# Normed attention's projections on steps of their own, and one wait for four scores

## The reference

```
k = _ln(x @ Wk.T), q = _ln(x @ Wq.T)      # per head of 16 numbers, 16 heads
v = x @ Wv.T
dot = einsum(q, k) / sqrt(16), causal mask
attn = softmax(dot);  out = einsum(attn, v) @ Wu.T
x = _layernorm(x + out)
```

## Time and profile before

| what | us |
|---|---|
| median of 3 executions | 4183.81 (4180.03 to 4212.95) |
| the profiled execution | 4193.01, its span 4191.2 |
| the stage, first transpose to last norm | about 1632 to 2144 of the span |
| its middle, from batch to batch 26 times | 1689.25 to 2085.85 |
| TensorE, VectorE, ScalarE busy over the span | 77%, 54%, 52% |

### The profile page before, as it was taken

The page is one execution under the profiler, slowest core; times in us unless marked ns, Lnnn a source line. Parts: engine busy times, 40 slices in busy tenths (PEclk is TensorE's granted clock), DMA queues, the critical chain, the costliest instruction groups (busy, mean ns, idle before and its releaser), DMA issues. The chain is left out here.

```text
span 4191.2 us, 84333 instructions
## 1 busy us (share of the span) xinstructions
PE 3225.6 (77%) x21166; PEld 1996.2 (48%) x21166; DVE 2278.8 (54%) x10359; ACT 2184.1 (52%) x6653; POOL 1448.4 (35%) x2228
## 2 busy tenths in 40 slices
PE   7999987888988824887767777877777775687772
PEld 5566665566666512444434444444444444344441
DVE  1222222566666684667648888888888882211112
ACT  3433333566566602666637877877777783221110
POOL 1111111355455545455523444444343441110005
PEclk9999998899999966768767887888888785899996
DMA  1000000111111011000010000000000003206773
GB/s 62 19 12 12 14 15 29 36 38 38 34 37 39 20 38 49 19 19 22 18 38 18 16 18 20 16 18 16 18 19 16 18 8 113 90 33 203 223 228 110
DMA packets 111870, 189.32 MB, mean 45 GB/s; under 512 B 11150, under 2 KB 95886, under 8 KB 105550
## 3 DMA queue, kind: packets, MB, share of 16 engines
q1 hardware_dynamic: 102094, 166.32, 12.9%
q10 hardware_dynamic: 7200, 14.68, 0.9%
q0 software_dynamic: 2400, 6.56, 0.5%
HBM read 149.90 MB, written 37.62 MB: 45 GB/s over the span
## 5 line engine op out<-in xcount | busy, mean ns | idle before, releaser
L3034 DVE MAX8 sa_cand<-sa_s 128x8 f32<-128x45 f32 (+3 forms) x3328 | 404.1, 191 | 34.7 <-ACT sa_s L2880 31.8
L852 ACT ACTIVATE ca_p<-ca_sm,ca_nb 100x361 f32<-100x361 f32 x512 | 301.9, 591 | 210.8 <-DVE ca_nb L936 209.8
L2763 PE MATMUL sa_tr<-sa_ident,sa_s 128*128 128x128 f32 (+3 forms) x1248 | 277.3, 339 | 167.9 <-POOL sa_s L2639 90.8
L672 POOL TENSOR_SCALAR ca_p<-ca_p,ca_rec 100x361 f32<-100x361 f32 x512 | 286.7, 579 | 345.2 <-DVE ca_rec L950 344.9
L2639 POOL TENSOR_SCALAR sa_s<-sa_s,sa_unit,sa_nu 128x361 f32<-128x361 f32 (+1 forms) x416 | 261.3, 644 | 306.3 <-DVE sa_nu L3126 306.3
L2763 PEld LDWEIGHTS sa_tr<-sa_ident,sa_s 128*128 128x128 f32 (+3 forms) x1248 | 185.5, 178 | 268.4 <-issue 257.5
L2888 ACT ACTIVATE sa_s<-sa_s,sa_nt 128x361 f32<-128x361 f32 (+1 forms) x416 | 244.3, 592 | 97.2 <-DVE sa_nt L3087 97.2
L936 DVE CUSTOM_DVE_ANT_0 ca_sm<-ca_sc,ca_mb 100x361 f32<-100x361 f32 x512 | 252.3, 526 | 69.4 <-PE ca_sc L759 56.4
L2896 ACT ACTIVATE sa_spare_a<-sa_s,sa_nu 128x361 bf16<-128x361 f32 (+1 forms) x416 | 247.2, 595 | 64.8 <-DVE sa_nu L3128 64.8
L2629 POOL TENSOR_TENSOR sa_over<-sa_cand,sa_tc 128x280 f32<-128x280 f32 (+3 forms) x128 | 99.3, 776 | 451.6 <-DVE sa_tc L3053 272.8
L2749 PE MATMUL sa_sc<-sa_kT,sa_qm 32*128 32x361 f32 (+3 forms) x768 | 227.2, 522 | 22.1 <-ACT sa_s L2880 21.5
(11 more groups left out here) (323 smaller groups left out, 7755.8 us busy)
## 6 DMA issues: line engine op xcount, KB each, us to landing
ea_we<-m_experts SPq DMA_DIRECT2D x40, 1024.0 KB, 6.6
ea_wd<-m_experts SPq DMA_DIRECT2D x40, 512.0 KB
ca_cTs<-cT SPq DMA_DIRECT2D x32, 361.0 KB
sa_cTs<-cT SPq DMA_DIRECT2D x32, 361.0 KB
rows_in<-me_zeros ACTq DMA_DIRECT2D x1, 7168.0 KB
ea_xe<-rows_in SPq DMA_DIRECT2D x40, 128.0 KB
rows_out<-ea_ye ACTq DMA_DIRECT2D x40, 128.0 KB
ca_ms<-mask SPq DMA_DIRECT2D x32, 141.0 KB
```

The source lines that it names most:

```text
L672: ins = pool.tensor_scalar(p[:, r, j, :], p[:, r, j, :], rec[:, r, j:j + 1], 1.0, ALU.mult, ALU.mult)
L852: act.activation(p[:, r, j, :], sm[:, r % 2, j, :], ACT.Exp, bias=nb[:, r % 2, j:j + 1], scale=-1.0, accum_out=den[:, r, j:j + 1]).then_in ...
L2763: mm = pe.transpose(tr[f % 2][0:kn, c0:c0 + rows], s[0:rows, u, i, k0:k0 + kn], ident[0:rows, 0:rows])
L3034: ins = dve.max(cand[0:rows, i, q, :], s[0:rows, u, i, PART[q]:PART[q + 1]])
```

## The change

Four things are changed, all in `normed_attention`. The projection of k and q moves from step 1 to step 0. The projection of v moves from the end of step 3 to the end of step 2, and its copy on ScalarE with it. The transpose of x moves from step 0 to the end of step 3 and works one batch further ahead (n+3 in place of n+2), for which the loads start a batch earlier and the written-out part of `passes` grows by a batch at the front and two at the back. And the four maxima of a step share one `stand`, on the last of the four scores.

```diff
             return (*shift(m, u, (r - steps) // 4), (r - steps) % 4)
 
         def passes(eng, body):
-            for n in range(-2, 2):
+            for n in range(-3, 2):
                 body(n // 2, n % 2)
-            with eng.Fori(1, B // 2 - 1) as m:
+            with eng.Fori(1, B // 2 - 2) as m:
                 body(m, 0)
                 body(m, 1)
-            for n in range(B - 2, B + 2):
+            for n in range(B - 4, B + 2):
                 body(n // 2, n % 2)
 
         block = ctx.enter_context(nc.Block())
@@ -1423,19 +1423,19 @@
                 sp.dma_start(out_s[n], xn[:, u, :]).then_inc(stored[u].sem, 16)
 
             def body(m, u):
-                if there(m, u, 4):
-                    load(*shift(m, u, 4))
+                if there(m, u, 5):
+                    load(*shift(m, u, 5))
                 if there(m, u, -3):
                     store(*shift(m, u, -3))
                 if there(m, u, 0):
                     load_residual(m, u)
 
-            for n in range(-4, 4):
+            for n in range(-5, 4):
                 body(n // 2, n % 2)
-            with sp.Fori(2, B // 2 - 2) as m:
+            with sp.Fori(2, B // 2 - 3) as m:
                 body(m, 0)
                 body(m, 1)
-            for n in range(B - 4, B + 3):
+            for n in range(B - 6, B + 3):
                 body(n // 2, n % 2)
             for u in range(2):
                 sp.wait_ge(*stored[u].at(B // 2, 0))
@@ -1484,6 +1484,7 @@
                 n = 2 * m + u
                 pe.wait_ge(*xq_in[u].at(m, 1))
                 pe.wait_ge(*v_done.at(n, -1))
+                pe.wait_ge(*xT_done.at(n, 0))
                 for k in range(KD):
                     mm = pe.transpose(mix[:, k * S:(k + 1) * S], xq[:, u, k * P:(k + 1) * P], ident[0:S, 0:S])
                 mm.then_inc(xt_done.sem, 1)
@@ -1505,9 +1506,9 @@
                     mm = pe.transpose(kq[:, k * S:(k + 1) * S], c[:, u, k * P:(k + 1) * P], ident[0:S, 0:S])
                 mm.then_inc(kqT_done.sem, 1)
 
-            def project_v(m, u, ahead):
-                n = 2 * m + u
-                if ahead:
+            def project_v(m, u):
+                n = 2 * m + u
+                if there(m, u, 1):
                     pe.wait_ge(*xT_done.at(n + 1, 1))
                 pe.wait_ge(*z_done.at(n, -2))
                 for k in range(KD):
@@ -1571,14 +1572,15 @@
                     if there(m, u, (r - 3) // 4):
                         values(*lag(m, u, r, 3))
                     if r == 0 and there(m, u, 2):
-                        turn_x(*shift(m, u, 2))
-                    if r == 1 and there(m, u, 2):
                         project_kq(*shift(m, u, 2))
                     if r == 1 and there(m, u, -2):
                         project_out(*shift(m, u, -2))
                     if r == 3 and there(m, u, 1):
                         scores(*shift(m, u, 1), 0)
-                        project_v(*shift(m, u, 1), ahead=there(m, u, 2))
+                    if r == 2 and there(m, u, 1):
+                        project_v(*shift(m, u, 1))
+                    if r == 3 and there(m, u, 3):
+                        turn_x(*shift(m, u, 3))
 
             passes(pe, sequence)
 
@@ -1648,12 +1650,12 @@
                         copy_kq(*shift(m, u, 1))
                     if r % 2 == 0 and there(m, u, (r - 2) // 4):
                         copy_turned(*lag(m, u, r, 2))
-                    if r == 0 and there(m, u, 2):
-                        copy_x(*shift(m, u, 2))
                     if r == 1 and there(m, u, 2):
                         squares(*shift(m, u, 2))
-                    if r == 3 and there(m, u, 1):
+                    if r == 2 and there(m, u, 1):
                         copy_v(*shift(m, u, 1))
+                    if r == 3 and there(m, u, 3):
+                        copy_x(*shift(m, u, 3))
 
             passes(act, sequence)
 
@@ -1686,8 +1688,8 @@
             def maxima(m, u, r):
                 n = 2 * m + u
                 dve.wait_ge(*exp_done.at(n, 4 * r - 12))
+                stand(dve, turns, *sc_done.at(n, 4 * r + 4))
                 for j in range(4):
-                    stand(dve, turns, *sc_done.at(n, 4 * r + j + 1))
                     dve.tensor_tensor_reduce(sm[:, r, j, :], sc[j][0:S, 0:S], cm[:, :], -1 / 4, 3e38, ALU.add, ALU.min,
                                              nb[:, r, j:j + 1]).then_inc(mx_done.sem, 1)
```

## The result

The changed kernel takes 4160.73 us (median of 5, 4154.11 to 4165.09) against 4186.78 us before (median of 5, 4180.03 to 4212.95). The ratio is 0.9927 with a 95% interval of 0.9899 to 0.9955. The forecast was 4148 us, within 4105 to 4192. In the profiled executions the span went from 4191.2 to 4163.3 us.

The account below looks back on a forecast made before the run. A chain to and fro between the engines sets the pace, with TensorE's clock varying. Legs summing to 13.7 to 14.5 us a batch gave 14.1, 36 us off over 31 steps: median 4148 us, range 4105 to 4192.

Parts of the forecast that it names:

- three legs: One batch's chain: first scores to k and q's projection, that projection, then on to the next first scores; 13.7 us half-low.
- One low spell a batch: TensorE's clock falls once a batch; the projection of k and q, first large work behind it, takes 2.5 to 3.5 us.
- the 14.1 chosen: Forecast us a batch in normed attention, the middle of 13.7 and 14.5, 1.15 less than now.
- half-low form: Case with half of k and q's projection at full clock and half at half clock: 13.7 us a batch.
- 0, with 3 us either way: Cost of the written-out batches' added code and some steps at the edges.
- The size of a set: Four maxima on VectorE, first to reciprocal, without register instruction and wait between: 0.74 us.
- the wait for the fourth score: At step 0 the first maximum starts 0.87 us behind the first scores, against 0.60 before; counts once a batch.
- waits were free: Rival, chance 0.06: VectorE's maxima keep their times but start on the fourth score; 14.65 us a batch, 4165 us.
- leg one: First scores to the start of k and q's projection: 3.3 or 3.8 us, 2.5 to 3.1 us off.
- Clock stays up: Rival, chance 0.27: TensorE's clock stays up more; 13.2 us a batch, 4121 us, or 4092 with no low spell.
- TensorE becomes the bound: Rival, chance 0.08: low clock lasts through the projections of k and q and of v; 16.5 us a batch, 4223 us.
- Nothing comes of it: Rival, chance 0.12: k and q's projection is wholly on the chain and new waits cancel gains; 15.25 us a batch, 4184.

Follow-up runs that it names:

- e7: Changed kernel plus two idle 256-column projections a batch, one behind v's projection, one behind the transpose of x; ratio 0.9828 to the kernel before, 12.15 us a batch.
- e10: e7 with a wait of its own for each of a step's four scores; ratio 0.9847 to the kernel before, 12.97 us a batch.
- e11: Kernel before, in its old order, with one wait a step and one idle 256-column projection ahead of step 3's transposes; ratio 0.9905, 13.39 us a batch.
- e1: Kernel before with only the one wait for a step's four scores, nothing moved; ratio 0.9945, 14.90 us a batch.
- e2: Changed kernel with all moves but four waits a step put back; ratio 1.0007 to the kernel before, 15.36 us a batch.
- e5: Changed kernel plus one idle 256-column projection behind v's projection, ahead of step 3's transposes; ratio 0.9944 to the kernel before, 13.68 us a batch.
- e3: Kernel before with one wait a step and only v's projection and copy moved to step 2; ratio 0.9950, 14.79 us a batch.

## Why the prediction was right, and where not

**The bound and the chain.** Right. A chain between the engines set the pace. Its walk came within 0.15 us in each of its three legs at the mixed clock (3.70 + 2.85 + 7.1, forecast 3.8 + 2.7 + 7.2) and within about 0.2 us at the full clock of e7 (3.09 + 1.89 + 7.13, forecast 3.3 + 1.8 + 7.2).

**The clock.** Right. One low spell a batch was expected and the projection of k and q to pay for it: it takes 2.92 to 3.74 us in the changed kernel. The mean, 13.83 us, lies below the 14.1 chosen, since nearly all batches stay in the half-low form. That the clock is the reason was shown by e7: more work, a clock of 1.00, and 1.7 us less a batch. By the rule of the Trainium skill (TensorE: Matmul & The Clock Gate, "Why this matters for your kernels") gaps this short leave the clock up. The trace does not agree: the longest wait of TensorE's matmuls in the list of the changed kernel is 1.3 us, and the projection of k and q still takes 2.92 us or more in every batch.

**The forecast on the median.** 36 us off was the sum. The stage gave 42.8, the rest of the program took 15 back: 14.1 in the sparse attention, 4 in the stages ahead, less 3 elsewhere. The prediction had priced the longer code at "0, with 3 us either way". That term was wrong in a way it had not looked at: the longer code cost nothing in its own stage's edges that shows, but 14.1 us in the next stage. Without them the profiled program would have gained 42 us and not 28. The 4 us ahead are most likely scatter: the first stage, which nothing touches, ends 3.6 us later, and over all profiled executions the first transpose of normed attention lies between 1627.7 and 1642.1 us. That the forecast came within 13 us of the median is in part luck, since the stage gave 7 us more than its 36 and the rest took 15.

**The maxima.** The size of a set, 0.74 us, was right, and the wait for the fourth score smaller than taken (0.73 us and not 0.87). What the waits cost was too small: the rival "waits were free" put 0.55 us a batch on them, e10 measured 0.82. The Trainium skill (VectorE: DVE Perf Modes, "Rules for kernel authors") says to minimise the number of operations, "not sems". e10 does not bear this out for these short operations; here three waits a step, each with its register instruction and its increment, cost 0.2 us, 0.07 us each. The runs don't tell these three apart.

**How the parts share the gain.** Here the reasoning fell short. The prediction added the parts up (2.5 to 3.1 us off leg one and 1.1 onto leg three, with the shorter maxima in both). In the experiments they don't add: in the stage 13.0 us for the one wait, 3.6 for the moves, 42.8 for both. Each shift of the chain also shifts how much of the projection meets the low clock, which the sum left out. It also took 2 us of v's projection as on the chain; at a full clock the whole of the moves is worth 0.1 to 0.3 us a batch (e11), so most of the 1.07 us a batch between e1 and the changed kernel comes through the clock (0.74 and 0.86). e1's expectation (5 to 10 us) and e2's (12 to 19 us lost) both missed, in part for that reason and in part because the waits cost more than taken: 24.4 us of the stage at a full clock (e10 against e7).

**The rivals.** "Clock stays up" and "TensorE becomes the bound" did not come, for the reasons given. "Nothing comes of it" came true for the moves alone (e2).

## What to carry to other kernels

Where TensorE's clock is near one of two levels by stretches, an order of work is worth what it does to the clock: look at which matmuls come first behind a gap. Matmuls without use in the gaps can pay (here 1.7 us of 13.8 a batch), so try that before a reordering, since it also tells how much the clock costs. And measure the parts together as well as alone: two changes of one chain need not add up. Last, look at the stages behind the changed one too: here 14 of the 43 us that the stage gained were lost there again, and 10 of them came back when VectorE's code was moved.

## What the runs showed that was not expected

- The clock fell although TensorE was busy 82% of the time and waited no longer than 1.3 us for another engine (1700 to 2050); with two projections of 256 columns more a batch it stayed at 1.00 throughout (e7).
- In the changed kernel batches settle at 13.62 to 13.77 us for ten or more in a row, in three executions, although the projection inside them could take from 1.8 to 3.7 us. The granted clock falls once in each of these batches, and the falls are as far apart as the batches are long (at 1709.2, 1722.8, 1736.5 and 1750.1 in the changed kernel). e5, with more work in each batch, settles at the same 13.62 to 13.77 us. Whether the clock's falls set the length of the batch was not tried.
- A stage that was not touched moved by 14 us with the place of VectorE's code, most of it by a stall once in each pass of its loop that went from 3.2 to 4.0 us; one packet of instructions moves in the short stalls and two in the long ones, in all 14 profiled executions.
- VectorE code that got shorter did no harm there: with the old order and one wait the sparse attention takes 1230.9 to 1231.1 us (e1, e3, e11).
